# The last chunk's softmax division: from token layout on TensorE to feature layout on VectorE, with its followers placed later

## The reference

```python
h = layernorm(x) * (1 + ca) + sa                      # per sequence
q, k, v = h @ Wq.T + bq, h @ Wk.T + bk, h @ Wv.T + bv  # 16 heads of 8
scores = einsum(q, k) * 8 ** -0.5 * exp(-alpha * |i - j|)
x = x + ga * (softmax(scores) @ v @ Wo.T + bo)
h = layernorm(x) * (1 + cb) + sb
shared = silu(h @ Sg) * (h @ Su) @ Sd
cw = top-2 of softmax(h @ Wr), 16 experts
x = x + gb * (shared + sum_e cw[e] * (silu(h @ Wg[e]) * (h @ Wu[e])) @ Wd[e])
```

## Time and profile before

| | us |
|---|---|
| median of 3 runs | 241.98 (241.18 to 242.21) |
| profiled execution | 242.38 |
| span of its instructions | 240.6 |

### The profile page before, as it was taken

The page is one execution under the profiler, slowest core; times in us unless marked ns, Lnnn a source line. Parts: engine busy times, 40 slices in busy tenths (PEclk is TensorE's granted clock), DMA queues, the critical chain, the costliest instruction groups (busy, mean ns, idle before and its releaser), DMA issues.

```text
span 240.6 us, 5812 instructions
## 1 busy us (share of the span) xinstructions
PE 226.1 (94%) x1830; PEld 166.3 (69%) x1830; DVE 194.1 (81%) x791; ACT 165.0 (69%) x333; POOL 182.7 (76%) x334
## 2 busy tenths in 40 slices
PE   7897999999899999899998999999999999999994
PEld 7765657665567675467775666777788888788882
DVE  3698897998998889999889988478746886966763
ACT  4457767699586999587977497586557659555550
POOL 6588898999997989897998979436576654675551
PEclk9999999999999999999999999999999999999999
DMA  5728905651007621007633640014324330037201
GB/s 142 219 50 195 312 8 122 171 148 47 1 3 173 183 83 48 1 3 166 169 106 118 204 132 0 3 63 158 90 92 128 106 120 0 0 118 207 89 32 44
DMA packets 16303, 24.38 MB, mean 101 GB/s; under 512 B 3281, under 2 KB 5969, under 8 KB 16145
## 3 DMA queue, kind: packets, MB, share of 16 engines
q1 hardware_dynamic: 15840, 24.01, 35.1%
q10 hardware_dynamic: 432, 0.01, 0.1%
HBM read 13.39 MB, written 1.18 MB: 61 GB/s over the span
## 4 chain that ended last, share of the span: by engine, by line
PE 59%; DVE 23%; ACT 8%; issue 5%; DMA 3%; SPq 2%; DVEq 0%; ACTq 0%
PE bank L926 59%; DVE sc L721 10%; ACT pr L408 2%; DVE attn_t L644 2%; DVE qk L636 1%; DVE mx L721 1%; DMA decay<-in_lag 1%; DMA qk_st<-qk 1%; ACT h_t L350 1%; ACT xn L363 1%; SPq L170 1%; DVE ex L682 1%; DVE sc L890 1%; DVE wgu_lo L742 1%; DVE qk_st L818 1%
## 5 line engine op out<-in xcount | busy, mean ns | idle before, releaser
L294 POOL TENSOR_SCALAR sc<-sc,mx 128x256 f32<-128x256 f32 x256 | 122.6, 505 | 11.1 <-DVE mx L721 10.8
L721 DVE CUSTOM_DVE_ANT_0 sc<-bank,decay 128x256 f32<-128x256 f32 x256 | 91.0, 418 | 10.8 <-PE bank L926 10.5
L408 ACT ACTIVATE pr<-bank 128x512 f32<-128x512 f32 x128 | 69.3, 596 | 24.0 <-PE bank L926 24.0
L926 PE MATMUL bank<-id_f,sc 128*128 128x128 f32 x512 | 69.1, 277 | 2.6 <-ACT pr L408 2.2
L338 POOL TENSOR_TENSOR act_lo<-sc,act_hi 128x512 fp32r<-128x512 f32 x35 | 45.2, 1294 | 34.4 <-ACT act_hi L576 34.4
L926 PEld LDWEIGHTS bank<-id_f,sc 128*128 128x128 f32 x512 | 55.7, 141 | 16.4 <-issue 8.3
L926 PE MATMUL bank<-pr,v_one 128*32 128x256 f32 x512 | 34.3, 385 | 0.0
L884 DVE TENSOR_TENSOR pr<-bank,cwb 128x512 f32<-128x512 f32 x32 | 22.0, 688 | 15.0 <-PE bank L926 14.9
L585 ACT ACTIVATE bank<-bank 128x512 f32<-128x512 f32 x32 | 18.6, 581 | 20.2 <-PE bank L926 19.9
L890 DVE TENSOR_TENSOR sc<-pr,bank 128x512 f32<-128x512 f32 x36 | 24.7, 687 | 6.3 <-ACT bank L585 2.9
L926 PE MATMUL bank<-h_hi,wgu_hi 128*128 128x512 f32 x72 | 28.8, 400 | 0.0
(11 more groups left out here) (110 smaller groups left out, 271.9 us busy)
## 6 DMA issues: line engine op xcount, KB each, us to landing
cwb<-cw_dram SPq DMA_DIRECT2D x64, 128.0 KB, 2.9
qk_st<-qk SPq DMA_DIRECT2D x60, 128.0 KB, 2.7
wgu_sb<-in_w_gu SPq DMA_DIRECT2D x1, 1152.0 KB, 5.8
wgu_sb<-in_x_t SPq DMA_DIRECT2D x4, 256.0 KB, 3.6
x_all<-in_x SPq DMA_DIRECT2D x1, 768.0 KB, 6.1
o_sum<-o_t SPq DMA_DIRECT2D x6, 128.0 KB, 2.3
o_val<-o_t SPq DMA_DIRECT2D x6, 128.0 KB, 2.2
out_dram<-wgu_sb SPq DMA_DIRECT2D x3, 256.0 KB, 3.2
```

The costliest lines, as they stand in the source:

```text
L294: last = nc.gpsimd.tensor_scalar(sc[:, n % RING, t, :], sc[:, n % RING, t, :], -1.0, mx[:, n % RING, t:t + 1], ALU.mult, ALU.add)
L408: nc.scalar.activation(pr[:, n % RING, :, :].rearrange("p a b -> p (a b)"), turn_bank(i, n)[:], ACT.Exp, scale=-1.0).then_inc(s["exp_done" ...
L721: last = nc.vector.tensor_tensor_reduce(sc[:, n % RING, t, :], ps_s[n % SB][:, t * SEQ:t * SEQ + SEQ], decay[:, t, :], float(HD) ** -0.5, ...
L926: return nc.tensor.matmul(o, l, r, start=start, stop=stop, skip_group_check=not check, is_transpose=transpose or None)
```

## The change

For chunk 3, `by_token`, `norm_tokens`, `attn_turn` and `attn_take` go, and with them the tiles `rsum` and `attn`. SP issues `move_rows` for chunk 3 as well, behind `weights_out(1)`. VectorE computes the inverse of `o_sum` in place in four pieces of 128 columns, one behind each of units 3 to 6 of the stage's chunk 0, then `norm`. The followers have new places, listed in the diff; chunk 2's weights_turn and weights_take move from unit 6 to unit 3, and `ln2t(2)` in chunk 3's quad 6 now waits for `cwt_ok` itself.

```diff
@@ sync
             weights_out(1)
+            for k in range(2):
+                move_rows(NCHUNK - 1, k)
@@ gpsimd
-                    if i == 0 and u == 7:
+                    if i == 1 and u == 1:
                         ln2_root(NCHUNK - 1)
                         ln2_shift(NCHUNK - 1)
@@ scalar
-            def attn_take(c):
-                act_e.wait_ge(s["at_done"], 1)
-                nc.scalar.activation(attn_t[:], ps_m[:], ACT.Copy).then_inc(s["at_ok"], 1)
...
                         if u == 3:
-                            attn_take(c)
-                        if u == 5:
-                            x2_take(c)
-                        if u == 6:
                             weights_take(c - 1)
                     if i == 1:
-                        if u < 2:
-                            xn_of(c, rstd2, nmr2, xn2, "nmr2_ok", "xn2_ok", ((0, 1), (2, 3))[u])
-                        if u == 4:
+                        if u == 0:
+                            x2_take(c)
+                        if u in (3, 4):
+                            xn_of(c, rstd2, nmr2, xn2, "nmr2_ok", "xn2_ok", ((0, 1), (2, 3))[u - 3])
+                        if u == 6:
                             h2(c)
-                        if u == 5:
+                        if u == 7:
                             h2_upper(c)
-                        if u == 7:
+                        if u == 8:
                             r_take(c)
                     if i == 2:
-                        if u == 1:
+                        if u == 2:
                             router_exp(c)
@@ vector
-            def norm_tokens(k):
...
+            def inverse_piece(t):
+                if t == 0:
+                    for k in range(2):
+                        dve.wait_ge(s_sums[k], 16 * NCHUNK)
+                at = slice(t * P, t * P + P)
+                last = nc.vector.reciprocal(o_sum[:, at], o_sum[:, at])
+                if t == TT - 1:
+                    last.then_inc(s["rec_ok"], 1)
...
                     if i == 0:
-                        if u == 1:
-                            norm_tokens(1)
                         if u == 0:
                             route_c(c - 1)
-                        if u == 4:
+                        if 3 <= u < 3 + TT:
+                            inverse_piece(u - 3)
+                        if u == 6:
+                            norm(c)
+                        if u == 8:
                             residual(c)
-                        if u == 6:
+                    if i == 1:
+                        if u == 1:
                             dve.wait_ge(s["x2_ok"], c + 1)
                             ln_stats(c, stats2, "stats2_ok")
                             ln_mean(c, stats2, mv2, "stats2_ok", "mv2_ok")
-                    if i == 1:
-                        if u == 6:
+                        if u == 8:
                             h2_lo_of(c)
-                        if u == 7:
+                    if i == 2:
+                        if u == 0:
                             route_a(c)
-                        if u == 8:
+                        if u == 1:
                             route_b(c)
-                    if i == 2 and u == 3:
-                        route_c(c)
+                        if u == 4:
+                            route_c(c)
@@ tensor
-            def by_token(c, k):
...
-            def attn_turn(c):
...
             def project_o(c):
-                if c < NCHUNK - 1:
-                    pe.wait_ge(s["norm_ok"], c + 1)
-                else:
-                    pe.wait_ge(s["at_ok"], 1)
+                pe.wait_ge(s["norm_ok"], c + 1)
...
-                if q == 6 and i:
-                    if nxt:
-                        pe.wait_ge(s["qk_lo_ok"], 2 * i + 4)
-                        res_turn(i - 1)
-                    else:
-                        pe.wait_ge(s["cwt_ok"], i - 1)
-                        by_token(i, 0)
+                if q == 6 and i and nxt:
+                    pe.wait_ge(s["qk_lo_ok"], 2 * i + 4)
+                    res_turn(i - 1)
...
                     if q == 6:
-                        pe.wait_ge(s["token_ok"], 1)
+                        pe.wait_ge(s["cwt_ok"], i - 1)
                         ln2t(i - 1)
...
                     if i == 0:
-                        if u == 1:
+                        if u == 3:
                             pe.wait_ge(s["lg_ok"], c)
-                            by_token(c, 1)
-                        if u == 3:
-                            attn_turn(c)
-                        if u == 4:
+                            weights_turn(c - 1)
+                        if u == 8:
+                            pe.wait_ge(s["cwt_ok"], c)
                             project_o(c)
+                    if i == 1:
+                        if u == 0:
+                            res_turn(c)
                         if u == 5:
-                            res_turn(c)
-                        if u == 6:
                             pe.wait_ge(s["x2_ok"], c + 1)
-                            weights_turn(c - 1)
-                    if i == 1:
-                        if u == 3:
-                            pe.wait_ge(s["cwt_ok"], c)
                             ln2t(c)
-                        if u == 6:
+                        if u == 7:
                             router(c)
```

More of the change, by code:

```diff
@@ L104, in build @@
         o_t = sb("o_t", [P, 2, CHUNK])
-        rsum = sb("rsum", [P, TT * QUAD, 2])
-        attn = sb("attn", [P, TT * QUAD, 2, HD, 2])
         o_val, o_sum = sb("o_val", [P, CHUNK]), sb("o_sum", [P, CHUNK])
@@ L129, in build @@
             "stats_ok mv_ok vare_ok rstd_ok nmean_ok nmr_ok xn_ok lnt_done h_ok qk_mm qk_hi_ok qk_lo_ok v_mm v_ok "
-            "s_done ttr_done nd_done t_done exp_done pv_done ot_ok c_done rs_ok token_ok ln_ok rec_ok norm_ok "
-            "at_done at_ok wo_done rt_ok rx_done x2_ok stats2_ok mv2_ok vare2_ok rstd2_ok nmean2_ok nmr2_ok xn2_ok ln2t_done "
+            "s_done ttr_done nd_done t_done exp_done pv_done ot_ok ln_ok rec_ok norm_ok "
+            "wo_done rt_ok rx_done x2_ok stats2_ok mv2_ok vare2_ok rstd2_ok nmean2_ok nmr2_ok xn2_ok ln2t_done "
             "h2t_ok h2hi_ok h2lo_ok r_done lg_ok top_ok fill_ok ls_ok struck_ok ex_ok zs_ok rz_ok em_ok "
@@ L749, in early @@
                     qk_lo_of(i + 1, 0, ps_m)
[L750 to L754, removed]
+                if i == NCHUNK - 1 and q == 3:
+                    norm(i - 1)
             def late(i, q):
@@ L994, in values @@
                 last.then_inc(s["pv_done"], 1)
-            def by_token(c, k):
-                pe.wait_ge(s["ot_ok"], 2 * c + k + 1)
-                transpose4(ps_m, o_t[:, k, :].rearrange("p (t k) -> p t k", t=TT)).then_inc(s["c_done"], 1)
-            def attn_turn(c):
-                pe.wait_ge(s["token_ok"], 2)
-                transpose4(ps_m, attn[:].rearrange("p (t j) l d h -> p t (j l d h)", t=TT)).then_inc(s["at_done"], 1)
             def project_o(c):
-                if c < NCHUNK - 1:
-                    pe.wait_ge(s["norm_ok"], c + 1)
-                else:
-                    pe.wait_ge(s["at_ok"], 1)
+                pe.wait_ge(s["norm_ok"], c + 1)
                 mm(ps_m[:], wa_sb[:, W_O, :], attn_t[:]).then_inc(s["wo_done"], 1)
```

## The result

The change made the kernel slower: 245.59 us at the median of 6 runs (244.52 to 246.57) beside 241.87 for the kernel before, a ratio of 1.0158 (1.0128 to 1.0187). In a second job it was 244.07 beside 240.78, 1.0111 (1.0063 to 1.0159). The medians are over all executions; the ratios leave out those disturbed by more than 1.5%, so a ratio is not quite the quotient of its two medians. The forecast of 244.0 has the right sign and the right three waits; the time of the first six runs lies above its range.

The account below looks back on a forecast made before the run. PE's own work was taken to bound the feed-forward stage. Waits of 3.8 us less 0.46 before, less 0.88 and 0.44 of PE's work, gave +2.0 us: 244.0 us, 8-in-10 range 242.7 to 245.3.

Parts of the forecast that it names:

- What bounds the kernel: In the feed-forward stage PE's own work was taken as the bound; three transpose groups leaving PE gain 1.32 us.
- Reciprocal: On VectorE, each 128-column piece was to take 0.94 us, 0.87 of its time, between 0.69 and 1.40.
- rival C: VectorE's reciprocals are dearer than the two-row line: 244.9 us at 1.2 a piece, 245.4 at 1.40; chance 0.2.
- First wait: PE before project_o, behind chunk 0's unit 8, for VectorE's norm held by POOL: 0.83 us, from 0 to 2.1.
- the walk: Unit-by-unit timing of the engines through the feed-forward stage, in the earlier kernel's clock, giving waits of 3.8 us.
- Second wait: PE before chunk 3's xn2 transposes, for POOL's root and shift behind act_lo 10, then ACT: 0.54 us, 0 to 1.
- Third wait: PE before weights_turn(3) in chunk 2's unit 5, for a late route_c held by POOL: 2.4 us instead of 0.34.
- The sum: Waits after 3.8 us, before 0.46, so +3.3; less 0.88 and 0.44 us of PE's work: +2.0 us.
- every new wait of PE is lost in full: In the feed-forward stage, PE has no other later wait that could give the time back; no size of its own.
- B: Only work taken off PE counts, POOL never in VectorE's way: 242.0 to 243.1 us, chance 0.13; gain over 1.2, 0.05.
- D: A VectorE product of two SBUF tiles is held back by several POOL operations: 1 to 2 us more; chance 0.07.

## Why the prediction was wrong, point by point

**What bounds the kernel.** Right: the stage is PE's, and the shorter list of PE is gained. From quad 6 to the stage 0.43 us (0.44 forecast; in all ten profiles with the changed attention 12.07 or 12.08 us, with the old one 12.51 or 12.52).

**Reciprocal.** VectorE's line through two rows gave 0.94 us for 128 columns. The tile view of o_sum, the last piece and norm, and GpSimd's act_lo 6 in the changed kernel:

```profile
L645 DVE RECIPROCAL o_sum<-o_sum x4: 944/944/946, 162.0 to 168.4; 128x128 f32<-128x128 f32 x4
...
168.38 0.94 DVE L645 RECIPROCAL o_sum<-o_sum 128x128 f32<-128x128 f32 x1
169.46 1.70 DVE L638 TENSOR_TENSOR attn_t<-o_val,o_sum 128x512 f32<-128x512 f32 x1
...
169.31 1.29 POOL L338 TENSOR_TENSOR act_lo<-sc,act_hi 128x512 fp32r<-128x512 f32 x1 [0.81 <-ACT act_hi L572]
```

It is 944 ns, and rival C with its 8 clocks a column is out. The repeat count of 8 in the Trainium skill (VectorE: DVE Perf Modes, "First, the fixed hardware budget") thus isn't the number of clocks per column here. 4, 32 and 128 columns took 178, 350 and 944 ns, 6.1 and 6.2 ns for each further one, where 8 clocks would be 8.3.

**First wait.** norm began 0.15 us behind act_lo 6, took 1.70 us, and ended 0.56 behind it: at 171.16, where the walk less 1.84 has 171.21. The wait was 0.58 and not 0.83, because PE itself arrived 0.2 us later than I had it.

**Second wait.** 0.51 for 0.54, by the forecast chain; the run with the root earlier shows it.

**Third wait.** ScalarE's table loads, then VectorE from act 21 on, and GpSimd:

```profile
200.35 1.28 ACT L444 ACT_TABLE_LOAD   x1
201.65 0.26 ACT L444 ACTIVATE ex<-ex 128x64 f32<-128x64 f32 x1
201.92 1.28 ACT L581 ACT_TABLE_LOAD   x1
203.22 0.58 ACT L581 ACTIVATE bank<-bank 128x512 f32<-128x512 f32 x1
...
203.89 0.69 DVE L881 TENSOR_TENSOR sc<-pr,bank 128x512 f32<-128x512 f32 x1 [1.19 <-ACT bank L581]
...
205.81 0.87 DVE L651 SCALAR_TENSOR_TENSOR wgu_sb<-bank,mod_t,wgu_sb 128x256 f32<-128x256 f32 x2
206.60 0.21 DVE L693 TENSOR_REDUCE zs<-ex 128x4 f32<-128x64 f32 x1
...
206.94 1.31 DVE L701 SCALAR_TENSOR_TENSOR cw<-struck,ex 128x64 f32<-128x64 f32 x1
208.28 0.22 DVE L707 TENSOR_TENSOR cw<-cw,rz 128x64 f32<-128x64 f32 x1
...
204.41 3.75 POOL L338 TENSOR_TENSOR act_lo<-sc,act_hi 128x512 fp32r<-128x512 f32 x3 [2.70 <-ACT act_hi L572]
```

act 21 at 203.9, the additions at 205.8 and route_c at 206.6 are each within 0.15 us of the walk (205.6, 207.55 and 208.3, less 1.84). Of its two operations that wait for GpSimd it was keep that stood from 206.94 to 208.25 and not the product, which changes the sum by 0.1. 2.68 measured, 2.41 forecast; by the walk's own two ends, 207.9 and 210.2, it should have been 2.3.

**The sum without the clock.** Stage 84.08 - 81.36 = +2.72 where the walk has +2.44, attention -0.43: +2.3 where I had +2.0. That would have been 244.3, in the range. The 0.12 us that the walk set down as a wait before the change, ahead of the old project_o, aren't in the trace (164.33 to 164.57, one matmul's distance); so the three waits less 0.34 are 3.43, less 0.88 of PE's work 2.55, and 0.17 of the 2.72 stay unexplained, within the pace that differs between traces.

**What failed** is a sentence of the first part: "every new wait of PE is lost in full". It was lost more than in full. The sum has no term for what PE does behind a wait; I read the granted clock of 1.00 as a constant, though no row of the kernel before has a gap in the stage beyond 0.34 us, so nothing there could have shown it. The third gap was forecast at 2.4 us and its consequence left out. It costs 1.35 us (1.57 by the run with the late route_c) in those executions in which it happens, 10 of the changed kernel's 16. With the fall the change thus costs 2.3 + 1.35 us, some 3.6, and five of the first job's six executions have it: their median is 3.7 above. With half of the executions falling, as in the second job, 3.0 are due, and there the medians differ by 3.3 and the ratio gives 2.7. Whether five of six and five of ten differ by chance or by the chip isn't shown, and no row could have told how often the clock would fall. The Trainium skill (TensorE: Matmul & The Clock Gate, "Why this matters for your kernels") says that idle gaps between bursts of matmuls bring PE's clock back to the lower level; it names gaps longer than most of those here. This case agrees on the fall, in 16 of 24 executions, and shows it already behind 2.02 us of idleness.

**What stays open.** Why the same gap brings the fall in one execution and not in the next. And why, in the second job, executions with a low clock are 2.35 us above the others where the fall costs 1.35: the start of the stage varied by 4 us among profiles of like kernels, and I have no trace of the executions at 246.5 us.

**Rivals.** B (no contention from GpSimd) didn't happen: norm and keep both stood behind a subtraction of GpSimd. The run with the pieces earlier shows how little it takes to spare norm that. C is out by its 944 ns. D didn't happen in this stage: no product of VectorE stood behind more than one operation of GpSimd, though in the attention stage norm still took up to 2.9 us.

## What to carry to other kernels

When work is taken off the bounding engine, price what its followers wait for, one by one, at their new places: here 1.3 us of PE's work was bought with 3.8 us of waits, and three moves by one unit each turned a loss of 1.1 to 1.6% into a gain of 0.3 to 0.5%. Give each forecast gap of PE of 2 us or more a second term, for the clock behind it, with a chance. And compare stages between two instructions of the same engine, since whole executions differ by more than the effect.

## What the runs showed of the hardware that I had not expected

- With a wait of 2.2 to 3.2 us of PE in the stage the span's mean granted clock was low in 16 of 24 executions, with matmuls put into the gap in 0 of 10. Two traces show the fall right behind the gap, to 1.2 GHz for some 3.4 us (0.57 and 0.52 in the windows): matmuls of 512 columns then start 0.43 us apart instead of 0.23, and the stage is 1.35 to 1.6 us longer.
- The same gap of 2.51 to 2.52 us of idleness had both outcomes in two profiles of one kernel, and one of 3.03 had none; behind a wait of 1.72 us for a DMA, early in the kernel, it fell as well, and behind one of 1.43 in the same place it didn't.
- A VectorE operation with two SBUF inputs that begins beside a GpSimd operation ends about 0.55 us behind that one's end if it has 512 columns (1.70 us), and takes 0.68 us alone. Of two short ones in a row (128x64) either may be the one that waits: 1.31 and 0.22 us in one trace, 0.19 and 1.20 in another.
